# A two-block transformer kernel: ternary weights through ScalarE, one small load, own buffers for the last group, new orders

## The reference, cut to what matters

```python
# layer 0: attention to ctx with rotary q and k, 8 heads of 64
x = x + tanh(g_xattn[0]) * (softmax(rope(xn @ Wq.T) . rope(ctx @ Wk.T)) @ (ctx @ Wv.T)) @ Wout.T
# layer 0: ternary feed-forward, hidden 2048
scale = clip(mean(abs(w), axis=1), 1e-5)            # one for each row of w
tern  = clip(round(w / scale), -1, 1)               # so w is used as tern * scale
h = bitlinear(xn, w_fc) + gate * (xn @ v.T @ fast_b.T @ u.T)
x = x + tanh(g_ffn[0]) * bitlinear(relu(h) ** 2, w_proj)
# layer 1: mixing with the mean of ctx, then a quantized feed-forward
x = x + tanh(g_xattn[1]) * (xn @ W1.T + mean(ctx @ W2.T) + b)
x = x + tanh(g_ffn[1]) * bitlinear(gelu(bitlinear(xn, w1, b1)), w2, b2)   # 8-bit activations, ternary w1 and w2
```

## Time and profile before

| | |
|---|---|
| median of 3 runs | 1259.27 us (1253.99, 1259.77, 1259.27) |
| profiled execution | 1254.16 us, span 1252.1 us |
| TensorE busy | 1120.1 us, 89% |
| VectorE busy | 975.9 us, 78% |
| ScalarE busy | 783.7 us, 63% |
| GpSimd busy | 577.6 us, 46% |
| moved by DMA | 140.28 MB |
| chain that ended last | PE 30%, DVE 27%, ACT 20%, DMA 11% of the span |

### The profile page before, as it was taken

The page is one execution under the profiler, slowest core; times in us unless marked ns, Lnnn a source line. Parts: engine busy times, 40 slices in busy tenths (PEclk is TensorE's granted clock), DMA queues, the critical chain, the costliest instruction groups (busy, mean ns, idle before and its releaser), DMA issues.

```text
span 1252.1 us, 19955 instructions
## 1 busy us (share of the span) xinstructions
PE 1120.1 (89%) x7102; PEld 697.7 (56%) x7390; DVE 975.9 (78%) x2029; ACT 783.7 (63%) x1509; POOL 577.6 (46%) x564
## 2 busy tenths in 40 slices
PE   5737788989999999999899999999999999999973
PEld 3525546565665656474656565575657465565631
DVE  5998877678779787978877888878876867877672
ACT  2588765758393947576485858385767657585622
POOL 3121465445564644554545455555545443644330
PEclk9757799999999999999999999999999999999997
DMA  9959843463625354444536362637354353524122
GB/s 312 348 141 319 224 117 73 71 130 64 128 54 135 65 113 86 102 98 100 118 64 143 62 142 51 125 66 127 73 95 108 66 115 61 108 58 81 30 59 51
DMA packets 302242, 140.28 MB, mean 112 GB/s; under 512 B 258097, under 2 KB 276017, under 8 KB 300465
## 3 DMA queue, kind: packets, MB, share of 16 engines
q1 hardware_dynamic: 299840, 136.62, 48.7%
q10 hardware_dynamic: 2304, 2.40, 0.6%
HBM read 57.97 MB, written 9.18 MB: 54 GB/s over the span
## 4 chain that ended last, share of the span: by engine, by line
PE 30%; DVE 27%; ACT 20%; DMA 11%; issue 6%; POOL 4%; SPq 2%; POOLq 0%; ACTq 0%; DVEq 0%
PE ps L1734 8%; ACT e L937 5%; PE ps L1782 4%; PE ps L1685 4%; PE ps L1718 3%; ACT rl L975 3%; PE ps L1770 3%; DVE st L1334 3%; DMA pt<-qT 3%; PE ps L1750 3%; ACT hid L980 2%; DVE qT L1347 2%; ACT sq L986 2%; DVE amax L1041 2%; DMA hT<-q 2%
## 5 line engine op out<-in xcount | busy, mean ns | idle before, releaser
L1718 PE MATMUL ps<-xT,fcT 128*128 128x256 f16 x2048 | 261.4, 276 | 7.1 <-ACT rl L975 7.1
L719 POOL TENSOR_TENSOR rs<-ve,nhalf 128x1 f32<-128x1 f32 x160 | 105.3, 660 | 321.7 <-DVE ve L1339 226.4
L1734 PE MATMUL ps<-pjT,hid 128*128 128x512 fp8e4 x1024 | 232.6, 380 | 2.6 <-issue 1.3
L1718 PEld LDWEIGHTS ps<-xT,fcT 128*128 128x128 fp8e4 x2048 | 202.2, 99 | 42.2 <-ACT rl L975 10.2
L744 POOL TENSOR_TENSOR hid<-sq,hid 128x512 f16<-128x512 f32 x128 | 155.9, 1221 | 114.0 <-ACT sq L986 113.6
L1734 PEld LDWEIGHTS ps<-pjT,hid 128*128 128x128 f16 x1024 | 97.7, 98 | 98.9 <-issue 1.3
L1782 PE MATMUL ps<-w2T,hT 128*128 128x512 fp8e4 x512 | 119.9, 389 | 23.0 <-DMA hT<-q 22.8
L975 ACT ACTIVATE rl<-ps,rsf 128x256 f32<-128x256 f32 x256 | 106.5, 469 | 43.5 <-PE ps L1722 43.5
L1770 PE MATMUL ps<-w1T,q4T 128*128 128x512 fp8e4 x512 | 122.9, 383 | 5.6 <-DMA q4T<-x16b 4.5
L1007 ACT ACTIVATE q<-h 128x2048 f16<-128x2048 f32 x32 | 61.1, 1909 | 104.4 <-DVE h L1491 104.4
L937 ACT ACTIVATE e<-ps,nmb,sig 128x128 f32<-128x128 f32 x256 | 113.1, 458 | 4.7 <-DVE nmb L1377 4.5
(11 more groups left out here) (207 smaller groups left out, 1998.8 us busy)
## 6 DMA issues: line engine op xcount, KB each, us to landing
xb<-in_x SPq DMA_DIRECT2D x16, 512.0 KB, 4.2
qS<-qT SPq DMA_DIRECT2D x128, 64.0 KB, 2.1
out<-r SPq DMA_DIRECT2D x32, 256.0 KB, 2.4
xa<-in_x SPq DMA_DIRECT2D x15, 512.0 KB, 4.4
rope<-in_rope SPq DMA_DIRECT2D x16, 384.0 KB, 3.4
h<-in_w1T SPq DMA_DIRECT2D x6, 1024.0 KB, 6.2
h<-in_w2T SPq DMA_DIRECT2D x6, 1024.0 KB, 6.4
h<-in_wkvT SPq DMA_DIRECT2D x2, 1024.0 KB, 16.1
```

The costliest lines, as they stand in the source:

```text
L1718: pe.matmul(dst, fcT[:, k, f * P:(f + 1) * P], xT2[:, xs, k, :], start=(xs == 0 and k == 0), stop=False)
L1734: mm = pe.matmul(ps[:, FFN0 + t, :], hid[:, xs, c, t * P:(t + 1) * P], pjT[:, c, :], start=(c == 0 and xs == 0), stop=(c == FC - 1 and xs ...
```

## The change

For the ternary weights: VectorE makes the reciprocal of each row's scale (`row_scales`; for `w_proj` the sum of absolute values is VectorE's too). ScalarE multiplies the piece in place by it and adds the constant 12582912 (`to_integers`), which rounds to an integer; TensorE transposes the float32 values, four blocks to a bank; ScalarE copies them out as the sign of the value less the constant (`evac`). The passes `is_gt` and `is_lt` with their buffers are gone. A place is free when the piece's last transposes are done (`used`).

Six small inputs are packed on the host into one array and loaded by one DMA; two row vectors and `u` are loaded by SyncE's queue.

For the last group (`final(g)`) the back stage has buffers of its own, which the front stages have finished with (`xb`, `xa`, `e`, `x16a`, `xT1`, `qT`, `hid`, `wo`, `wq`), and the PSUM banks of the attention. Its waits for the group before are gone. Gelu, square, maximum, rounding and integer pass go by quarters of 512 columns, and the transpose by halves.

The tables `ORDER` and `PREP` are new throughout. In the last group ScalarE now has both gelus ahead of both integer passes. For most groups the places moved by a few.

```diff
@@ the preparation
-            def evac(q):
-                for a in range(2):
-                    act.wait_ge(c_tern, 2 * q + a + 1)
-                    src = ps[:, 5 + a, :].bitcast(F16)
...
-                    act.activation(dst, src, ACT.Copy, scale=-1.0, saturate=False).then_inc(c_quantp, 1)
+            def to_integers(q):
+                act.wait_ge(c_thr, q + 1)
+                src = piece[PLACE[q]]
+                for a, b, scale in scale_parts(q):
+                    last = act.activation(src[:, a:b], src[:, a:b], ACT.Copy, scale=scale, bias=MAGIC)
+                last.then_inc(c_quant, 1)
+            def evac(q):
+                for a in range(KC):
+                    act.wait_ge(c_tern, KC * q + a + 1)
+                    src = ps[:, 5 + a % 2, :]
...
+                    act.activation(dst, src, ACT.Sign, bias=drop[:, :], saturate=False).then_inc(c_quantp, 1)
@@ def used
-                eng.wait_ge(c_quant, n + 1)
+                eng.wait_ge(c_tern, KC * (n + 1))
@@ vector engine
-            def thresholds(q):
...
-            def signs(q):
...
+            def row_scales(q):
...
+                    dve.tensor_reduce(sc, piece[PLACE[q]], axis=AX.X, op=ALU.add, apply_absolute_value=True).then_inc(c_rowd, 1)
...
+                dve.reciprocal(rsc[:, cols], sc).then_inc(c_thr, 1)
@@ def ternary
-                for a in range(2):
-                    if q >= 1:
-                        pe.wait_ge(c_quantp, 2 * q + a - 1)
-                    for n in range(8 * a, 8 * a + 8):
+                for a in range(KC):
+                    if q > 0 or a >= 2:
+                        pe.wait_ge(c_quantp, KC * q + a - 1)
+                    for n in range(4 * a, 4 * a + 4):
                         src = (n % KC) * D + (n // KC) * P if kind == "fc" else n * P
-                        mm = pe.transpose(ps[:, 5 + a, :].bitcast(F16)[:, n % 8 * P:(n % 8 + 1) * P],
-                                          neg[q % 2][:, src:src + P], ident16[:, :])
+                        mm = pe.transpose(ps[:, 5 + a % 2, n % 4 * P:(n % 4 + 1) * P], piece[PLACE[q]][:, src:src + P],
+                                          ident[:, :])
@@ small loads
-            for dst, src in ((mask[:, :], mask_d), (vT_sb, ...), (fb_sb, fb_d), ... (bxbc[:, :], ...)):
-                act.dma_start(dst, src).then_inc(d_small, 16)
-            act.dma_start(uT, uT_d).then_inc(d_u, 16)
+            act.dma_start(small[:, :], small_d).then_inc(d_small, 16)
@@ the last group
+        def final(g):
+            return g == GROUPS - 1
+        def mix_bank(g, n):
+            return att_bank(n) if final(g) else back_bank(n)
...
+            def gelu_quarters(g, t):
+                for n in range(4):
+                    need(act, h_done, 4 * TILES, g, 4 * t + n)
+                    c = slice(n * 512, (n + 1) * 512)
+                    act.activation(h_of(g)[:, t, c], h_of(g)[:, t, c], ACT.Gelu).then_inc(gelu, 1)
+                for n in range(4):
...
+                    act.activation(q5_of(g, t)[:, c].bitcast(BF16), h_of(g)[:, t, c], ACT.Square,
+                                   accum_out=ssq_n[:, t, n:n + 1]).then_inc(sqsum, 1)
+            def int_quarters(g, t):
+                need(act, sqsum, TILES, g, 4 * t + 3)
...
@@ def turn_q5
+                if final(g):
+                    for half in range(2):
+                        need(sp, q5_done, TILES, g, 4 * t + 2 * half + 1)
+                        sp.dma_start_transpose(hT_of(g)[:, t, half * 8:half * 8 + 8, :],
+                                               q5_of(g, t)[:, half * 1024:half * 1024 + 1024])
...
@@ PREP, the preparation's places
-            PE=dict(k=(1, 2), v=(3, 4), low=(7,), mix=(11,), tern=(5, 18, 19, 20, 21, 23, 25, 26), low_t=(22,),
+            PE=dict(k=(2, 3), v=(4, 5), low=(0,), mix=(10,), tern=(14, 15, 17, 20, 23, 25, 27, 30), low_t=(19,),
-                     evac=(22, 25, 29, 33, 36, 38, 41, 44), rows=(3, 4, 9, 12, 14, 15, 16, 18), low=(37,), wx=(32,),
-                     sums=(30, 35, 39, 42, 45, 46, 47, 49), lift=(51, 52, 56, 58, 62, 75, 76, 82)),
+                     evac=(21, 27, 30, 34, 37, 40, 44, 47), rows=(4, 5, 8, 18),
+                     whole=(6, 7, 10, 20, 25, 28, 36, 46), low=(33,), wx=(38,),
+                     sums=(39, 42, 45, 48, 53, 54, 55, 57), lift=(68, 75, 76, 79, 82, 83, 88, 93)),
```

More of the change, by code:

```diff
@@ L791, in prepare @@
                     pool.memset(lowF, 0.0).then_inc(c_lowzero, 1)
-                for q in here("POOL", "above", p):
-                    if q in ON_POOL:
-                        signs_above(q)
             def run():
@@ L1004, in q5_int @@
+            def int_quarters(g, t):
+                need(act, sqsum, TILES, g, 4 * t + 3)
+                for n in range(4):
+                    need(act, q5_round, TILES, g, 4 * t + n)
+                    c = slice(n * 512, (n + 1) * 512)
+                    act.activation(q5_of(g, t)[:, c], h_of(g)[:, t, c], ACT.Copy, bias=-MAGIC).then_inc(q5_done, 1)
             def q5_int(g, t):
```

626 lines of the change are left out of this document (340 added, 286 removed), and 132 rows, old and new, of tables (down, exp, h, hid).

## The result

The changed kernel takes 1221.72 us, the kernel before 1256.63 us beside it: ratio 0.9738, 95% interval 0.9707 to 0.9769. Measured again beside later experiments its ratio was 0.9749 (0.9730 to 0.9768). The forecast was 1242 us with a range from 1228. The forecast started from 1259.3 us; beside the changed kernel and beside the experiments the kernel before took 1253 to 1257 us.

A forecast was written before the change was run, and what follows sets the result against it. TensorE was taken to bound the middle groups, so gains could come only from preparation, first up stage and tail. Head -8.1 and tail -8.8 gave -17 us, from 1259.3 to 1242 us; 8-in-10 range 1228 to 1257.

The forecast's parts named there:

- The middle: Fourteen middle groups, bound by TensorE: other orders, same work; taken as 0, its idle time moving 4 us either way.
- (1): Head: the first exponential, before at 74.17 us, starts 6.5 us earlier; bounds 0 and 10.
- (2): Head, ScalarE from the first exponential to x2's second high part: 6.9 us more, mainly evacuations and whole passes.
- C: Rival: a float32 transpose is two passes at full clock, 0.5 us; head +6, tail -9: 1256 us; chance 0.12.
- D: Rival: a float32 transpose is two passes at slow clock, 0.8 us; head +23, tail -9: 1273 us; chance 0.08.
- (3): Head, first up stage, before 27.8 us: 6 us shorter, with one lift and two sets of exponentials there.
- (4): Head, 160 to 201 us: 2.5 us less TensorE standstill, group 2's q going ahead of x3's transposes.
- The head's sum: Preparation to second up stage: -6.5 + 6.9 - 6 - 2.5 = -8.1 us.
- The small loads: Six small loads on ScalarE's queue joined into one: taken as zero, bounds -2 and +1 us.
- (5): Front of the tail: TensorE's new order brings group 15's x2 earlier; gain 2.5 us, bounds 0 and 5.
- (6): Tail behind the last h: last w2 ends 22.6 us after it, before 28.9; gain 6.3 us, bounds 4 and 9.
- The sum: Whole kernel: head -8.1 and tail -8.8 make -17 us, from 1259.3 to 1242.

## Why the prediction was wrong

**The middle, the step that failed.** "The middle: other orders, same work; its idle of 12.4 us in 260 can move by 4 us either way. I take 0." It moved by 13, and in the kernel before with nothing but these orders changed. The mechanism, that TensorE bounds the middle, was right and is what hid the gain: I took "bound by TensorE" for "nothing to gain". In the whole stretch of 908 us TensorE stood 38.6 us, and nothing excluded that an order closes a quarter of that. The bound should have been the idle time itself, and more. Beside the 9 us of idle time, some 4 us more come without any idle time in the records: the same products fill a little less busy time. Their ends are modelled, so I can't say by what.

**(1) The first exponential.** Forecast 6.5 us earlier, bounds 0 and 10; it came 11.5 and 9.7 us earlier in two traces. VectorE was the path, as the step said, but with less slack than it gave: put back, 23 us of passes ahead of the first exponential make it 17 to 19 us later.

**(2) ScalarE up to x2.** Forecast 6.9 us more between the first exponential and x2's second high part; 3.9 and 5.4 in the two traces (before 48.2 us, from 74.17 to 122.40; then 52.1 and 53.6). The evacuations waited 4 us in all for the transposes. Rivals C and D fall with that: eight float32 transposes take 1.04 us at full clock and 1.97 at half, as single passes (rows in the last section), where C had 0.5 us for one and D 0.8.

**Between (2) and (3), a term that the sum does not have.** From x2's second high part to the first up product it is 12.2 us in place of 9.5, since TensorE waits 8.64 us for x2's transposes (the row at 124.50) where it waited 3.77:

```profile
129.35 2.72 PE L1698 MATMUL ps<-xT,vrep 128*128 128x256 f16 x12 [3.77 <-DMA xT<-x16f]
```

That is 2.8 us in this trace and 0.0 to 2.7 in the other seven; what makes these transposes land later was not shown.

**(3) The first up stage.** Forecast -6; it took 18.6 us in place of 27.5, -8.9.

**(4) From the first up stage to the second.** Forecast -2.5; it was +8.3 (41.5 us before, 49.8 after), the largest error of sign. The step priced the moved lifts at zero, since the first w1 comes late enough. It named the price, "each lift on the path would cost 2 us", but looked only at who needs the result, not at what stands behind the weight passes on ScalarE and VectorE: group 1's attention. What fits the experiments above is that the chain of weight pieces then sets the end of the stretch.

The head's sum, -8.1, is near the 8 us that the experiments leave for it and the 5.5 us at group 1's up stage (-11.5 + 3.9 + 2.8 - 8.9 + 8.3). That is luck, since its errors cancel: 14 us gained by 146 us, 8 of them given back.

**The small loads**: nothing, as forecast.

**(5) The tail's front**: forecast 2.5, bounds 0 and 5; 2 to 3 by the experiment, 5 by the traces at equal work.

**(6) The end.** Forecast H + 22.6, bounds 19.7 and 25; it was H + 18.9. The term that was mis-sized is the rate of the last sixteen products: the forecast had 0.393 us each as before, but they ran at 0.227 (3.63 / 16), 2.7 of the 3.7 us. The other 1.0 is that they start at H + 15.3 and not at H + 16.3. Before, they came behind idle times of 12.24 and 6.11 us, at a granted clock of 0.72 from 1220 us on the earlier trace rows; now they follow the first tile's `w2` after 0.94 us, and from 1210 us on the granted clock is 1.00. The forecast had this case as a bound (0.216 us each, H + 19.7) and did not take it. What freed the second tile was named rightly, the wait for the first one's transpose; how little the quarters do beside it was not.

**The sum.** Head 8 (8.1), middle 13 (0), tail 11 (8.8): 32 us in place of 17; since the head is what the two others leave, this adds up by construction. Of the 20 us between 1242 and 1221.72 the middle is 13 and the tail 2. The other 5 or so are mostly the starting value: the forecast took 1259.3 us for the kernel before, which took 1256.63 beside the changed one and 1253.1 to 1254.2 beside the experiments, near the profiled 1254.16 that it had set aside as the lower of two clusters. With the middle alone put right it would have been 1229 us, inside its range.

## What to carry over

When a kernel's steps are put in a new order, look at the bounding engine's idle time over the whole stretch for what that can give, not at the idle time's scatter in one window: of 38.6 us in 908 the new orders took 9 here, where the engine was 96% busy, and 4 us more came beside it. What a wrong order costs has no such bound: one seam cost TensorE 10.4 us at once. Price a moved pass by what stands behind it on its own engine, not only by who needs its result; if moving a step away from a wait only moves the wait to the next product, look for the slow chain underneath. Don't read a gain of 3 us off one milestone of one trace: the same orders put it over 5 us apart here. Before splitting a tile into quarters, try the own buffer and the order that uses it: they gave eight of ten us here.

## What the hardware showed

Float32 transposes run as single passes, and each takes twice as long as a float16 one at the same clock. At full clock eight float32 ones take 1.04 us (the row at 73.99 us above) and eight float16 ones of the kernel before 0.62; at a granted clock of 0.50 eight float32 ones take 1.97 us, and sixteen float16 ones 1.87:

```profile
71.10 1.97 PE L1642 MATMUL ps<-ident,hT 128*128 128x128 f32 x8 [7.61 <-ACT fcT L902]
```

```profile
99.89 0.62 PE L1559 MATMUL ps<-ident,r 128*128 128x128 f16 x8 [0.22 <-ACT pjT L862]
```

Less the length of the last record of each (0.27, 0.22, 0.42 and 0.31 us), one float32 transpose follows another after 0.11 us at full clock and 0.22 at half, a float16 one after 0.06 and 0.10. A float32 product was recorded as two passes; at full clock a pass over 512 columns took 0.44 us in the kernel before:

```profile
23.71 7.03 PE L1588 MATMUL ps<-h,r 128*128 128x512 f32 x16
```

So a float32 product costs some 0.22 us for 128 columns (7.03 / 16 x 2 / 4, an estimate), twice a transpose. The Trainium skill, TensorE: Matmul & The Clock Gate, in its glossary entry on xbus, gives the transpose mode as four times faster for FP32 on trn2; the trace agrees in direction, with a factor of two against a product. The forecast's 0.25 us is near the half-clock value. Its bound of 0.12 came from float16 rows at half clock and matches the float32 rows at full clock by chance.

Sign needs no table of its own here. Between 60 and 201 us the changed kernel's ScalarE runs 32 passes of Sign among its exponentials, and the first table load behind the one at 2.21 us is that of the gelu:

```profile
226.28 1.28 ACT L1036 ACT_TABLE_LOAD   x1
```

The Trainium skill, ScalarE: Activation LUTs, section on table sets, says that cheap functions stand in every set as filler; the forecast had left open whether Sign is one of them, and the trace says that one loaded set serves it and Exp.
